# A message-passing kernel: the loop over further tiles is moved and partly taken apart

## The reference, cut to what matters

```python
h = x                                       # 3125 nodes x 128
for _ in range(5):                          # first part: a gated network
    agg = segment_sum(h[dst] @ W_msg.T + b_msg, src)
    h = gru(agg, h)
x = layernorm(x + h)
z, e = x, None                              # second part: three edge layers
for We, be, Wn, bn in layers:
    parts = [z[src], z[dst]] + ([e] if e is not None else [])
    e = relu(concatenate(parts, -1) @ We + be)         # 50000 edges x 128
    agg = segment_sum(e * edge_weight[:, None], dst)
    z = relu(concatenate([z, agg], -1) @ Wn + bn)
x = layernorm(x + z)
```

## Time and profile before

| | |
|---|---|
| median of 3 runs | 2152.61 us (2151.59 to 2153.83) |
| the profiled execution's own time | 2155.89 us |
| its span in the trace | 2153.6 us |
| busy: PE, DVE, POOL, ACT | 1842.1, 1384.0, 984.5, 658.3 us |
| mean granted PE clock | 0.934 |
| pass 1 / 2 / 3 begin at | about 855 / 1264 / 1701 us |

### The profile page before, as it was taken

One profiled execution on the slowest core, in us unless ns is written; L12 is line 12 of the kernel. 1 busy time (PEld: TensorE's weight loads), 2 busy tenths in 40 slices (PEclk: granted clock), 3 DMA queues, 4 the chain that ended last, 5 costly groups with the idle time before them and its releaser, 6 DMA issues. The chain is left out here.

```text
span 2153.6 us, 47982 instructions
## 1 busy us (share of the span) xinstructions
PE 1842.1 (86%) x14363; PEld 1426.2 (66%) x14363; DVE 1384.0 (64%) x4563; ACT 658.3 (31%) x1271; POOL 984.5 (46%) x1025
## 2 busy tenths in 40 slices
PE   5777689999999994588888876999999969999985
PEld 2332244545454544488877766999999769999983
DVE  8998621313131325499888864777777648888775
ACT  1378811212121212233333332333333311121112
POOL 2000067720000000477777734777777357777770
PEclk7888799999999996799999988999999979999997
DMA  3146810030000004455544544777777435555551
GB/s 101 46 93 111 109 13 3 2 6 0 0 0 0 0 0 159 149 160 156 153 151 148 149 121 127 221 226 227 224 226 226 149 96 150 150 157 150 153 149 37
DMA packets 193777, 242.14 MB, mean 112 GB/s; under 512 B 56404, under 2 KB 120175, under 8 KB 192927
## 3 DMA queue, kind: packets, MB, share of 16 engines
q1 hardware_dynamic: 161151, 172.73, 29.1%
q0 software_dynamic: 31840, 57.21, 11.2%
q10 hardware_dynamic: 576, 9.44, 1.1%
HBM read 149.76 MB, written 69.88 MB: 102 GB/s over the span
## 5 line engine op out<-in xcount | busy, mean ns | idle before, releaser
L1332 POOL DMA_INDIRECT rows<-p_dram,src_i x864 | 831.8, 963 | 359.1 <-issue 239.4
L1912 DVE TENSOR_TENSOR agg_t<-psum,agg_t 128x128 f32 x1380 | 393.3, 285 | 153.8 <-PE psum L1780 127.0
L976 PE MATMUL psum<-adj,parts 128*128 (+2 forms) x1750 | 339.7, 351 | 6.2 <-ACT agg L1056 4.4
L1845 ACT ACTIVATE rows<-rows 128x512 f32<-128x512 f32 x216 | 136.2, 630 | 593.0 <-DVE rows L1905 593.0
L1896 DVE TENSOR_SCALAR hot_w<-col_f,dst_loc,weight 128x128 f32<-128x128 f32 x864 | 305.6, 359 | 0.8
L976 PEld LDWEIGHTS psum<-adj,parts 128*128 128x128 f16 x1750 | 153.0, 98 | 191.9 <-issue 23.4
L1760 PE MATMUL psum<-w_c,before 128*128 128x128 f32 x1840 | 261.0, 286 | 0.0
L841 POOL DMA_INDIRECT records<-record_of,place_i x128 | 126.2, 986 | 268.7 <-issue 268.7
L924 DVE SCALAR_TENSOR_TENSOR gate_room<-psum,b_h,gate_room 128x512 f32<-128x512 f32 (+1 forms) x35 | 23.9, 683 | 348.2 <-ACT gate_room L1063 348.2
L1745 PE MATMUL psum<-p_sb,pair_src 128*128 x1032 | 153.3, 296 | 94.3 <-issue 44.2
L1780 PE MATMUL psum<-hot_w,rows 128*128 128x128 f32 x1728 | 232.1, 278 | 0.0
(11 more groups left out here) (252 smaller groups left out, 2359.1 us busy)
## 6 DMA issues: line engine op xcount, KB each, us to landing
e_dram<-after SPq DMA_DIRECT2D x230, 256.0 KB
before<-e_dram SPq DMA_DIRECT2D x230, 256.0 KB
adj<-stage SPq DMA_DIRECT2D x196, 97.8 KB, 4.0
pair_rows<-sorted_rows SPq DMA_DIRECT2D x129, 128.0 KB
rows<-p_dram,src_i POOLq DMA_INDIRECT x864
hot_all<-dst_rows ACTq DMA_DIRECT2D x2, 3072.0 KB, 14.9
p_dram<-p_sb SPq DMA_DIRECT2D x9, 512.0 KB
records<-record_of,place_i POOLq DMA_INDIRECT x128, 2.1
```

What stands on the lines that cost most here:

```text
L976: mm = nc.tensor.matmul(psum[:, AGG_BANK, 0:n_cols], parts[:, w, part, :], adj[:, w, cols], start=(w == 0 and part == 0), stop=(w == WINDO ...
L1332: nc.gpsimd.indirect_dma_start(out=rows[:, b % ROW_SLOTS, m * D:(m + 1) * D], out_offset=None, in_=p_dram, in_offset=bass.IndirectOffsetOn ...
L1845: nc.scalar.activation(e_of(q), source, ACT.Relu).then_inc(e_on, 1)
L1912: nc.vector.tensor_tensor(a, psum[:, A_BANKS[q % len(A_BANKS)], m * P:(m + 1) * P], a, ALU.add).then_inc(agg_on, 1)
```

## The change

Four parts, the same in each pass. POOL runs its loop (`further_rows`) ahead of its first quad's gathers. SP loads the first record as the pass's first DMA. PE runs its loop (`further_tiles`) ahead of slot 0. DVE makes the index, the number and the one-hots of the first further tile at the very start of its program, and those of the next turn at the end of each turn of its loop, behind a wait for the next record.

```diff
@@ -1645,9 +1645,8 @@
             node.gpsimd(pool)
+            further_rows()
             for b in range(REST_QUADS):
-                if b == ROWS:
-                    further_rows()
                 if b >= ROWS:
                     pool.wait_ge(summed, slot_of(b - ROWS) + 1)
@@ -1669,11 +1668,11 @@
+            sp.dma_start(over_rec[:], keep["records"][SORT_TILES * P:(SORT_TILES + 1) * P, :]).then_inc(over_rec_in, 16)
             if is_first:
                 node.sync(sp)
             for i in range(LOADED):
                 load_pair(i)
-            sp.dma_start(over_rec[:], keep["records"][SORT_TILES * P:(SORT_TILES + 1) * P, :]).then_inc(over_rec_in, 16)
@@ -1806,7 +1805,7 @@
-                if q == 2:
+                if q == 0:
                     further_tiles()
@@ -1912,6 +1911,16 @@
+            def further_hots():
+                nc.vector.tensor_copy(over_src[:], over_rec[:, 3:4]).then_inc(over_hots_on, 1)
+                nc.vector.tensor_copy(over_win[:], over_rec[0:1, 4:5]).then_inc(over_hots_on, 1)
+                nc.vector.tensor_scalar(over_hot, keep["col_f"][:], over_rec[:, 1:2], None,
+                                        ALU.is_equal).then_inc(over_hots_on, 1)
+                nc.vector.tensor_scalar(over_hot_w, keep["col_f"][:], over_rec[:, 1:2], over_rec[:, 2:3],
+                                        ALU.is_equal, ALU.mult).then_inc(over_hots_on, 1)
+
+            dve.wait_ge(over_rec_in, 16)
+            further_hots()
             if is_first:
                 dve.wait_ge(keep["sorted_got"], 32)
@@ -1927,13 +1936,6 @@
             with dve.Fori(0, overflow(mybir.EngineType.DVE)) as i:
-                dve.wait_ge(over_rec_in, i * 16 + 16)
...
                 dve.wait_ge(over_hots_on, i * 4 + 4)
@@ -1944,6 +1946,8 @@
                 dve.wait_ge(over_agg_on, i + 1)
+                dve.wait_ge(over_rec_in, i * 16 + 32)
+                further_hots()
```

## The result

| | before | after |
|---|---|---|
| median, same chip | 2153.22 us (4 runs) | 2113.95 us (4 runs) |
| span in the trace | 2153.6 us | 2111.7 us |
| pass 1 | 408.7 us | 399.6 us |
| pass 2 | 437.5 us | 422.5 us |
| pass 3 | 419.5 us | 400.8 us |

A forecast was written before the change was run, and what follows sets the result against it. POOL's row gathers bound passes 1 and 3, PE's steps pass 2, after early stalls on the further tile. Gains of 10.65 + 15.2 + 15.2 = 41.1 us from 2155.9, less 3.3 for the median, gave 2111.5 us, range 2104 to 2122.

The forecast's parts named there:

- POOL's 17th gather: The further tile's row gather in each pass; in pass 3 PE stood 10.53 us for it, forecast gone.
- POOL's fifth quad: POOL's gathers that need the sum of step 1; in pass 3 forecast to start 15.2 us earlier.
- PE's step 3: PE's fourth quad of tiles, needing a load of "before"; in pass 2 forecast 15.2 us earlier.
- The load in pass 2: SP's load of "before" for step 3, forecast to land at 1304.2, PE still waiting 1.6 us.
- in pass 1 POOL could lose 3 us more before it feels it: Slack in pass 1 for DVE's wait for the second record at its loop's end; cost forecast zero.
- rival C: Second record and SP's loop hold DVE or loads 5 us longer in passes 2 and 3: 2121.5 us, chance 0.12.
- `pair_dst` as PE's releaser at step 3: Sign of being wrong: PE's step 3 released by DVE's pair one-hots, whose delay was forecast to cost zero.
- A row lands about 3.5 us after issue: Further row's time from POOL's gather to landing; in pass 3 forecast there at some 1723.4, before PE can begin.
- Step 2 and the sum of step 0 take 5.0 us: PE's work at pass 3's head after the further tile, forecast to end at 1739.9.
- rival B: PE, no longer standing, runs at its faster rate from step 2 on: 47.5 us gained, 2105 us, chance 0.10.
- the loop count's load: Run-time count load standing open ahead of POOL's first gather; 0.56 us taken, bounds 0 and 1.4 us.
- Rivals D and E: D, slower: the stall was cover, 2158.5 us, chance 0.03; E, no change: something else holds the row, 2152.6, chance 0.03.

The follow-up runs named there:

- e1: The changed kernel with only POOL's part undone, its loop again behind the first four quads' gathers: 2152.7 us, ratio 0.9993 to the kernel before.
- e10: The change itself run and profiled again, nothing edited, on the same chip as e9: ratio 0.9811 to the kernel before, 41 us below it.
- e5: The changed kernel with hot_all's last 3 MB load asked for later in pass 1, behind ACT's slot 7: ratio 0.9817 to the kernel before.
- e9: e8 without e5's edit, PE loading the count behind the stage's products, where it stands idle: ratio 0.9765 to the kernel before, 51 us below.
- e2: The changed kernel with only PE's part undone, its loop ahead of slot 2 again: 2126.8 us, ratio 0.9873 to the kernel before.
- e7: The changed kernel with SP's next record loaded earlier and POOL's and PE's loop counts ahead of the stage's waits: ratio 0.9798 to the kernel before.
- e8: e7 and e5 together, plus the next layer's weights asked for behind SP's slot 12: ratio 0.9791 to the kernel before, 45 us below.

## Why the prediction was right

The forecast was 2111.5 us and 41.1 us gained; measured were 2113.95 and 39.3. Its picture held in passes 2 and 3, and in pass 1 but for two links: the stall of each pass was PE waiting for POOL's 17th gather (e1), and the gain is read at POOL's fifth quad in passes 1 and 3 and at PE's step 3 in pass 2, since POOL and PE are full behind these points. Ahead of the further row's relu PE's wait fell under 1 us in passes 2 and 3, as announced, and was 1.4 us in pass 1 (3.62 in e10). The load in pass 2 was late as said, by 3.5 us and not 1.6.

That the total came out so near is in part luck. By passes the forecast was 10.65, 15.2 and 15.2 us, and measured were 9.1, 15.0 and 18.7: pass 3's surplus covers pass 1. Four sizes were off, and partly cancelled.

- *"in pass 1 POOL could lose 3 us more before it feels it"*: DVE's wait for the second record in pass 1 was to be covered. The store on SP took 6.7 us and not 2, in the shadow of a 3 MB load (e5), and the head of the pass won 5.9 instead of 9.3 us. This is rival C, but in pass 1, not in passes 2 and 3, and `pair_dst` as PE's releaser at step 3 was announced as a sign of being wrong.
- *"A row lands about 3.5 us after issue"*: in pass 1 it took 6.1 us, and 8.2 in e10, since the gather now stands next to the 3 MB load; 3.6 us without it (e5). The length had been read where the load was over. The prediction weighed a row 2.5 us late in pass 1, for DVE's work beside POOL; it was late by about that, but for the load. It cost PE 0.7 us more than in the other passes, 2.9 in e10, and part of that came off the wait at step 3.
- *"Step 2 and the sum of step 0 take 5.0 us"*: they took 2.5, as rival B had it. The 5.0 us came from a PE that had just stood, with a granted clock of 0.50; now it is 1.00 there. With the loop's head 0.7 us longer than said, pass 3's head still won 16.2 instead of 15.2 us.
- *"the loop count's load"*: 0.56 us for POOL was 1.1 to 1.4, the upper bound. In e9 about 0.7 of it went.

Rivals D and E are out: no pass is longer, and e1 shows what it looks like when the row comes no earlier. Open is pass 3's remainder. From the fifth quad on it took 362.2 us before and 359.7 after, 2.5 us that I had not forecast; but e1, with the gather in its old place, took 359.1 and e2 363.0, so it is not shown to belong to the change. The same goes for 1.9 of the 3.2 us of pass 1.

## What to carry to other kernels

A rare piece of work is dear where its one slow step stands in a queue behind the bulk, and where other engines meet it in their strict order. Put the slow step first, make what it needs before that, and then look who waits in the piece's loop with ordinary work queued behind: here PE's loop two slots earlier, which frees SP's loads, was worth some 13 us more. Look too at what transfers run at the new place: in pass 1 the early gather met a large load that the late one had missed. After such a move, look at waits for things that nobody needs yet (the record of a turn that never comes), and load run-time counts where the engine stands idle anyway, not at the head of a stage (e7 and e8 show the cost of the second; e9 doesn't show the gain of the first by itself).

## What the runs showed of the hardware that was not expected

- A 64 KB store to DRAM by SP landed in 2.3 us with no large load beside it (e5), and in 4.4 and 6.7 us in two profiles beside a 3 MB load on ACT's queue. A gather of 128 rows on POOL landed in 3.6 us without that load (e5), and in 6.1 and 8.2 us in the same two profiles with it; where the gather had a start of 1.75 us on the load, in 3.7 (e7).
- The slow products behind PE's stalls are its granted clock, at 0.50 (1.2 GHz) instead of 1.00. In pass 3 of the kernel before, the eight products at 1725.54 took 2.07 us with the clock at 0.50, and those at 1763.24, in the midst of work, 1.06 with the clock at 1.00. With the change the clock is 0.50 in the window 1701 to 1711, and the eight products at 1706.42 took 1.92 us; in 1711.3 to 1721.5 it is 1.00, and those at 1715.23 took 1.06. This fits what the Trainium skill says in "TensorE: Matmul & The Clock Gate", Part 1, that half rate is the state at rest and activity lifts it.
- A pause of 2.12 us ahead of ten 512-column products was followed by a granted clock of 0.73 over them, and they took 6.25 us (e8, pass 2; 2.10 and 6.25 in e7). Behind pauses of 0.93 to 1.64 us the clock was 1.00 and they took 4.53 to 4.55.
